# A graph and attention layer on one Trainium2 core: x's transposes in eight PSUM banks, edge slots in three pieces

## The chip, the core and the metric

The kernel runs on one core of one Trainium2 chip. The metric is the device time of one execution in microseconds (us). Three timed runs of the kernel before gave 1199.53, 1200.68 and 1201.06 us, median 1200.68.

## What is computed

`x` has 625 rows of 768 numbers. One layer is computed: a layer norm, a graph convolution over 20,625 edges, an attention of 12 heads with 266 random features, an output projection, and then a mixture of 16 experts in which each row uses one shared expert and up to three chosen ones. The change touches only the beginning. Cut to that, the reference is:

```python
xn = layernorm(x)
deg = segment_sum(ones, dst); norm = deg**-0.5[src] * deg**-0.5[dst]
gnn = segment_sum((xn @ gnn_W)[src] * norm, dst) + gnn_b
q, k, v = split(xn @ W_qkv)
q1, k1 = softmax_features(q), softmax_features(k)
mix = (q1 @ (k1.T @ v)) / (q1 @ sum(k1)) @ W_proj + b_proj
x = x + gnn + mix
x = x + experts(layernorm(x))
```

## The kernel before, in words

There is no scheduler: each engine (PE, ACT, DVE, POOL, SP) has its own list of instructions, written by hand, and the engines wait for each other on semaphores. Every product is made of three matmuls, (high, high), (high, low) and (low, high): ACT copies a matrix to a rounded high half and DVE subtracts that to get the low half (`split_high`, `split_low`, L499 to L508).

**Transposes of x.** After the norm, PE transposes xn into PSUM in eight groups: six groups "c" with the first four row tiles of one 128-column chunk, and two groups "l", ("l", 0) and ("l", 4), with the last row tile of four and of two chunks (`turn_tokens`, L462). ACT copies each group to `xhi` (L1380, L1383), then DVE subtracts it to `xlo` (`x_lower`, L973) and frees its bank. `groups` (L321) gives each key a bank in turn, out of the list it is handed; `fill` (L396) makes PE wait, before it writes a group into a bank, until the use before it has been freed. The x groups share banks 5, 6 and 7. Behind them PE transposes two small things, `lnrow` (group "lt", L1628) and `prow` (group "pt", L1634), and then starts the product h = xn @ gnn_W (`rows_times("h")`, L1659 to L1676), in two halves s of five row tiles. `rows_times("v")` follows in the same form, and then the columns of k (`columns_times`, L1678). The matmuls of the second half of v need `split_low(dve, "v", 1)`.

**Edge slots.** Each of 125 partitions holds 165 edges. DVE marks each edge's bucket of 25 (`ehot`), runs a scan over the marks (`erun`, L896), and sends totals to PE, which sums them (`bucket_ranks`, L1652, between the fourth and the fifth group of h). From PE's answer DVE makes each edge's slot in a table: `slots_of(a, b)` (L918) does so for columns a to b of the 165, with 25 instructions into `epos`, one reduction (L925), nine small instructions in a chain, each waiting for the one before (`link`), the last of which is the copy to `eslot` (L935) that raises `eslot_ok`. POOL then scatters the 165 columns into DRAM, one indirect DMA each (L731), and waits for `eslot_ok` before the first column of each piece. SP waits for it too, before it loads W_q. DVE's order in this stretch is:

```python
slots_of(*HALVES_OF_EDGES[0])
split_low(dve, "v", 0)
slots_of(*HALVES_OF_EDGES[1])
tile_regions()
split_biases()
split_low(dve, "v", 1)
```

The scattered table is loaded back (L640) long after, when PE projects the attention's output, and DVE makes one-hot matrices of it (L963) from which PE counts the adjacency matrix.

Of the kernel before, what the change touches and what calls it, by code (L numbers as in the profile page):

```python
# [31 lines left out]
ET = EDGES // TP  # L32
# [4 lines left out]
EDGE_RANGE = 32768.0  # L37
IN_FLIGHT = 8
WARM = 92
FIRST_EDGES = 28  # L40
HALVES_OF_EDGES = [(0, FIRST_EDGES), (FIRST_EDGES, ET)]
OFFSETS = 16
REGION = [512 * (r // 4) + TP * (r % 4) for r in range(BUCKETS)]
COUNT_BANKS = (BUCKETS + 3) // 4
# [65 lines left out]
def gps_kernel(nc, x, src, dst, gnn_w, gnn_b, w_qkv, w_proj, b_proj, proj_mat, gate_w, gate_b,  # L110
# [3 lines left out]
    with ctx:  # L114
# [206 lines left out]
        def groups(keys, banks):  # L321
            nonlocal turn
            for key in keys:
                b = banks[turn % len(banks)]
                turn += 1
                uses[b] += 1
                plan[key] = (b, uses[b])

        R3, R8 = [5, 6, 7], list(range(8))
        T8 = [("c", c) for c in range(C)] + [("l", 0), ("l", 4)]  # L330
        groups([("xt",) + k for k in T8], R3)
        groups([("lt", 0)], R3)
        groups([("pt", 0)], R3)
        groups([("h", i, s) for s in range(2) for i in range(NT)], R3)
# [80 lines left out]
        def sems(names):  # L415
            return [sem(n) for n in names.split()]
# [15 lines left out]
        iota_r_ok, epad_ok, etot_ok, eslot_ok, eoffs_ok, bias_ok, eye_ok, oh_ready, oh_free, counted, adj_ok, adjsum_ok = sems(  # L432
            "iota_r_ok epad_ok etot_ok eslot_ok eoffs_ok bias_ok eye_ok oh_ready oh_free counted adj_ok adjsum_ok")
# [18 lines left out]
        def done(eng, key):  # L452

            b, n = plan[key]
            eng.wait_ge(full[b], n)
# [48 lines left out]
        def split_low(dve, name, s):  # L504

            dve.wait_ge(half_hi, HALVES.index((name, s)) + 1)
            dve.tensor_tensor(wlow[name][:, :, 384 * s:384 * s + 384], wraw[name][:, :, 384 * s:384 * s + 384],
                              high_half(name, s)[:, :, :].bitcast(F32), ALU.subtract).then_inc(half_lo, 1)  # L508
# [67 lines left out]
        def _(sp):  # L576
# [6 lines left out]
            def load_qkv(name, a):  # L583
                sp.dma_start(wraw[name][:, :, :], w_qkv.rearrange("(c p) n -> p c n", c=C)[:, :, a:a + D]).then_inc(ld_w[name], 16)
# [14 lines left out]
            sp.dma_start(bias_f[:, F // 8:], fc2_b.rearrange("e (j c) -> (e j) c", j=8)).then_inc(ld_bf, 16)  # L599

            done(sp, ("xt", "l", 4))
            sp.wait_ge(eslot_ok, 2)
            load_qkv("q", 0)
            sp.wait_ge(eoffs_ok, 1)
            sp.dma_start(region_dram.rearrange("(p w) -> p w", p=128), eoffs[:, :]).then_inc(st_offs, 16)
# [85 lines left out]
        def _(pool):  # L691
# [31 lines left out]

            pool.wait_ge(st_epad, 16)
            for k in range(ET):
                for n, (a, b) in enumerate(HALVES_OF_EDGES):
                    if k == a:
                        pool.wait_ge(eslot_ok, n + 1)
                if k >= IN_FLIGHT:
                    pool.wait_ge(st_edges[k % IN_FLIGHT], 16 * (k // IN_FLIGHT))  # L730
                pool.indirect_dma_start(out=edge_dram, out_offset=bass.IndirectOffsetOnAxis(ap=eslot[:, k:k + 1], axis=0),  # L731
                                        in_=epair[:, k, :].bitcast(I32), in_offset=None).then_inc(st_edges[k % IN_FLIGHT], 16)
# [126 lines left out]
        def _(dve):  # L859
# [46 lines left out]
            def edge_slots():  # L906

                ps = read(dve, ("er", 0))
                link(dve.tensor_scalar(etiles[:, :], ps[:, 32:32 + BUCKETS], 1.0 / 128, 127.0 / 128 - 0.5 + 0.5 / 128, ALU.mult, ALU.add))
                link(dve.tensor_scalar(etiles[:, :], etiles[:, :], ROUND, ROUND, ALU.add, ALU.subtract))  # L910
                link(dve.tensor_tensor_scan(eend[:, :], ones[:, 0:BUCKETS], etiles[:, :], 0.0, ALU.mult, ALU.add))
                link(dve.tensor_tensor(efrom[:, :], eend[:, :], etiles[:, :], ALU.subtract))
                emptied(dve.scalar_tensor_tensor(out=efrom[0:TP, :], in0=efrom[0:TP, :], scalar=EDGE_RANGE, in1=ps[0:TP, 0:BUCKETS],
                                                 op0=ALU.mult, op1=ALU.add), ("er", 0))
                taken(dve, ("er", 0))
                link(dve.tensor_tensor(efrom[0:TP, 1:BUCKETS], efrom[0:TP, 1:BUCKETS], elast[:, 0:BUCKETS - 1], ALU.subtract))

            def slots_of(a, b):  # L918

                for n in range(BUCKETS):  # L920
                    last = dve.scalar_tensor_tensor(out=epos[:, n, a:b], in0=erun[:, n, a:b], scalar=efrom[0:TP, n:n + 1], in1=ehot[:, n, a:b],
                                                    op0=ALU.add, op1=ALU.mult)
                link(last)
                value, base_of, quo_of = evalue[:, a:b], ebase[:, a:b], equo[:, a:b]
                link(dve.tensor_reduce(value, epos[:, :, a:b].rearrange("p b k -> p k b"), AX.X, ALU.add))  # L925

                link(dve.tensor_scalar(base_of, value, 1.0 / EDGE_RANGE, -0.5 - 0.5 / EDGE_RANGE, ALU.mult, ALU.add))
                link(dve.tensor_scalar(base_of, base_of, ROUND, ROUND, ALU.add, ALU.subtract))
                link(dve.scalar_tensor_tensor(out=value, in0=base_of, scalar=-EDGE_RANGE, in1=value, op0=ALU.mult, op1=ALU.add))
                link(dve.tensor_scalar(quo_of, value, 1.0 / 128, -0.5 - 0.5 / 128, ALU.mult, ALU.add))  # L930
                link(dve.tensor_scalar(quo_of, quo_of, ROUND, ROUND, ALU.add, ALU.subtract))
                link(dve.scalar_tensor_tensor(out=base_of, in0=quo_of, scalar=1.0 - 128 * ET_TILES, in1=base_of, op0=ALU.mult, op1=ALU.add))
                link(dve.scalar_tensor_tensor(out=value, in0=value, scalar=float(ET_TILES), in1=base_of, op0=ALU.mult, op1=ALU.add))
                link(dve.tensor_scalar(value, value, -float(ET_TILES), None, ALU.add))
                dve.tensor_copy(eslot[:, a:b], value).then_inc(eslot_ok, 1)  # L935
# [68 lines left out]
            bucket_totals()  # L1004
            split_low(dve, "h", 1)
            edge_slots()
            slots_of(*HALVES_OF_EDGES[0])
            split_low(dve, "v", 0)
            slots_of(*HALVES_OF_EDGES[1])
            tile_regions()  # L1010
            split_biases()
            split_low(dve, "v", 1)
# [1025 lines left out]
```

## Time and profile before

| | |
|---|---|
| median of three runs | 1200.68 us |
| profiled execution, own time | 1206.77 us |
| its span | 1205.1 us |
| mean granted PE clock | 0.979 |
| PE busy | 1151.7 us (96%) |
| DVE busy | 761.0 us (63%) |
| ACT busy | 659.1 us (55%) |
| POOL busy | 490.4 us (41%) |

The profiled execution's own time is 1.67 us above its span and 6.09 us above the median of the timed runs. All the rows further down are of that execution. The first 30 us are the norm and x's transposes, 30 to 63 us the product h, 63 to 95 us v, 95 to 190 us k, q and their features, 190 to 316 us the attention, 316 to 385 us the output projection with the counting of the edges, and the experts fill the rest.

### The profile page before, as it was taken

The numbers are of one execution on the slowest core, as the hardware profiler recorded it, in microseconds if no ns is written. First come the engines' busy times: TensorE is split into PE (matmuls) and PEld (weight loads), VectorE is DVE, ScalarE is ACT, GpSimd is POOL, SyncE is SP. The second block draws the span as 40 slices with busy tenths as digits, with TensorE's granted clock in tenths as the row PEclk, the third lists the DMA queues.
The fourth block names the chain that finished last, engine by engine and source line by source line (L and its number), as shares of the span: only waits on it lengthen the run. The fifth ranks groups of instructions, "written<-read, shape, count | busy, mean of one in ns | idle before, by whom it ended". The sixth has DMA issues, their size and how long they took to land.

```text
span 1205.1 us, 20725 instructions
## 1 busy us (share of the span) xinstructions
PE 1151.7 (96%) x6465; PEld 1014.8 (84%) x6493; DVE 761.0 (63%) x1191; ACT 659.1 (55%) x1040; POOL 490.4 (41%) x340
## 2 busy tenths in 40 slices
PE   6999999999889999999999999999999999999985
PEld 5999898777666678888999988888889989998874
DVE  7862643256487656525866865747675896666973
ACT  3222673155500145336876684857776977486953
POOL 1188888788811000443632521312443642222511
PEclk8999999799999999999999999999999999999988
DMA  9030005140300330146596574565775959377933
GB/s 311 17 88 2 3 2 142 26 163 2 82 13 3 104 116 28 27 116 212 223 350 231 188 291 148 207 205 187 300 272 204 373 183 336 86 279 282 349 115 98
DMA packets 63089, 191.71 MB, mean 159 GB/s; under 512 B 14316, under 2 KB 15383, under 8 KB 63045
## 3 DMA queue, kind: packets, MB, share of 16 engines
q1 hardware_dynamic: 51316, 172.86, 39.3%
q0 software_dynamic: 11728, 18.27, 8.5%
q8 instruction: 27, 0.44, 0.2%
q14 instruction: 18, 0.14, 0.0%
HBM read 178.74 MB, written 15.09 MB: 161 GB/s over the span
## 4 chain that ended last, share of the span: by engine, by line
PE 81%; DVE 5%; ACT 4%; DMA 4%; issue 3%; POOL 1%; ACTq 0%; SPq 0%; DVEq 0%; another core or an unknown queue 0%; POOLq 0%
PE banks L1939 25%; PE banks L1923 23%; PE banks L1672 5%; PE banks L1689 4%; PE banks L1739 3%; PE banks L1837 3%; PE banks L1859 3%; PE banks L1704 3%; PE banks L1907 3%; PE banks L1761 2%; PE banks L1911 2%; DMA out<-ysb,sidx 2%; ACT kfeat L1432 2%; PE banks L1900 1%; PE banks L1750 1%
## 5 line engine op out<-in xcount | busy, mean ns | idle before, releaser
L731 POOL DMA_INDIRECT edge_dram<-epair,eslot x165 | 224.4, 1360 | 99.4 <-issue 99.4
L795 POOL DMA_INDIRECT out<-ysb,sidx x27 | 126.3, 4679 | 233.1 <-issue 198.6
L521 ACT ACTIVATE w2hi<-w2raw 128x1536 fp32r<-128x1536 f32 x96 | 139.1, 1483 | 90.2 <-DMA w2raw<-in_L_ffn_fc_w 80.0
L534 DVE TENSOR_TENSOR w2lo<-w2raw,w2hi 128x1536 fp32r<-128x1536 f32 x96 | 164.5, 1753 | 25.9 <-ACT w2hi L521 23.8
L1939 PE MATMUL banks<-w2hi,hthi 128*128 128x384 f32 x624 | 161.8, 340 | 0.1
L1939 PE MATMUL banks<-w2hi,htlo 128*128 128x384 f32 x624 | 159.2, 336 | 0.0
L1939 PE MATMUL banks<-w2lo,hthi 128*128 128x384 f32 x624 | 158.9, 335 | 0.0
L521 ACT ACTIVATE w1hi<-w1raw 128x1536 fp32r<-128x1536 f32 x96 | 137.6, 1495 | 29.2 <-DMA w1raw<-in_L_ffn_fc_w 25.7
L534 DVE TENSOR_TENSOR w1lo<-w1raw,w1hi 128x1536 fp32r<-128x1536 f32 x80 | 144.1, 1865 | 0.0
L1923 PE MATMUL banks<-w1hi,xthi 128*128 128x512 f32 x486 | 139.7, 396 | 2.6 <-POOL w1lo L534 2.6
L1923 PE MATMUL banks<-w1lo,xthi 128*128 128x512 f32 x486 | 136.9, 390 | 0.0
L1923 PE MATMUL banks<-w1hi,xtlo 128*128 128x512 f32 x486 | 136.6, 389 | 0.0
L1525 ACT ACTIVATE hid<-banks,lnwb 128x128 f32<-128x128 f32 x324 | 116.0, 488 | 32.2 <-PE banks L1907 31.1
L867 DVE BATCH_NORM_STATS2 st<-hid 128x6 f32<-128x512 f32 x81 | 50.7, 681 | 117.8 <-ACT hid L1536 117.8
L1939 PEld LDWEIGHTS banks<-w2lo,hthi 128*128 128x128 f32 x624 | 113.5, 189 | 0.0
L1939 PEld LDWEIGHTS banks<-w2hi,htlo 128*128 128x128 f32 x624 | 113.0, 188 | 0.0
L1939 PEld LDWEIGHTS banks<-w2hi,hthi 128*128 128x128 f32 x624 | 111.8, 189 | 0.6 <-issue 0.6
L1923 PEld LDWEIGHTS banks<-w1lo,xthi 128*128 128x128 f32 x486 | 91.3, 188 | 19.3
L1923 PEld LDWEIGHTS banks<-w1hi,xtlo 128*128 128x128 f32 x486 | 91.3, 188 | 19.2
L1923 PEld LDWEIGHTS banks<-w1hi,xthi 128*128 128x128 f32 x486 | 89.0, 188 | 19.8 <-POOL w1lo L534 2.2
L1211 DVE TENSOR_TENSOR htlo<-hid,hthi 128x1536 fp32r<-128x1536 f32 x26 | 45.7, 1756 | 85.4 <-ACT hthi L1531 85.4
L534 POOL TENSOR_TENSOR w1lo<-w1raw,w1hi 128x1536 fp32r<-128x1536 f32 x16 | 60.2, 3765 | 28.9 <-remote 17.2
(347 smaller groups left out, 1867.8 us busy)
## 6 DMA issues: line engine op xcount, KB each, us to landing
w1raw<-in_L_ffn_fc_w SPq DMA_DIRECT2D x96, 768.0 KB
w2raw<-in_L_ffn_fc_w SPq DMA_DIRECT2D x96, 768.0 KB, 6.6
xs<-in_x SPq DMA_DIRECT2D x10, 336.0 KB
edge_dram<-epair,eslot POOLq DMA_INDIRECT x165
wg<-in_L_gnn_W SPq DMA_DIRECT2D x1, 2304.0 KB, 12.6
wv<-in_L_mix_W_qkv SPq DMA_DIRECT2D x1, 2304.0 KB, 13.8
wk<-in_L_mix_W_qkv SPq DMA_DIRECT2D x1, 2304.0 KB, 17.7
wq<-in_L_mix_W_qkv SPq DMA_DIRECT2D x1, 2304.0 KB, 9.0
```

The costliest lines, as they stand in the source:

```text
L521: act.activation(unit(w2hi if second else w1hi, second, u), unit(w2raw if second else w1raw, second, u), ACT.Copy).then_inc(w2_hi if secon ...
L534: eng.tensor_tensor(unit(w2lo if second else w1lo, second, u), unit(w2raw if second else w1raw, second, u), unit(w2hi if second else w1hi, ...
L731: pool.indirect_dma_start(out=edge_dram, out_offset=bass.IndirectOffsetOnAxis(ap=eslot[:, k:k + 1], axis=0), in_=epair[:, k, :].bitcast(I3 ...
L795: pool.indirect_dma_start(out=out, out_offset=bass.IndirectOffsetOnAxis(ap=sidx[:, 0:1], axis=0), in_=ysb[:, :], in_offset=None, bounds_ch ...
L867: last = dve.bn_stats(st6[0:p, n, :], rows[:, n * step:(n + 1) * step])
L1211: dve.tensor_tensor(lo[:, :, :].rearrange("p c t -> p (c t)"), hid[:, :], hi[:, :, :].rearrange("p c t -> p (c t)").bitcast(F32), ALU.subt ...
L1525: last = act.activation(hid[:, 128 * c:128 * c + 128], tr_ps[c // 4][:, 128 * (c % 4):128 * (c % 4) + 128], ACT.Identity, scale=lnw[:, bas ...
L1672: last = pe.matmul(ps[0:TP, 0:384], a[:, c, t], w, start=c == 0 and k == 0, stop=c == C - 1 and k == 2)
L1689: last = pe.matmul(ps[:, 0:b - a + b % 2], w, xt_[:, c, a:b + b % 2], start=c == 0 and k == 0, stop=c == C - 1 and k == 2)
L1704: filled(pe.matmul(ps[0:TP, 0:M], of[r:r + HD, h // 2, TP * i:TP * i + TP], projt[r:r + HD, :], start=True, stop=True), (name, i, h))
L1923: last = pe.matmul(hid_ps[n][:, :], a[:, c, :], w[:, c, 512 * n:512 * n + 512], start=c == 0 and k == 0, stop=False)
L1939: last = pe.matmul(y_ps[s][:, 0:384], a[:, c, :], w[:, c, 384 * s:384 * s + 384], start=c == 0 and k == 0, stop=False)
```

## The change

The eight groups of x's transposes get banks 0 to 7, one each. The second piece of the edge slots, columns 28 to 165, is split in two, 28 to 96 and 96 to 165, one right behind the other; POOL waits at columns 0, 28 and 96, and SP's wait before the load of W_q is for the third piece. One line fewer stands at the top of the file, so the lines from 41 to 1006 have numbers lower by one.

```diff
-FIRST_EDGES = 28
-HALVES_OF_EDGES = [(0, FIRST_EDGES), (FIRST_EDGES, ET)]
+PARTS_OF_EDGES = [(0, 28), (28, 96), (96, ET)]
...
-        groups([("xt",) + k for k in T8], R3)
+        groups([("xt",) + k for k in T8], R8)
...
-            sp.wait_ge(eslot_ok, 2)
+            sp.wait_ge(eslot_ok, len(PARTS_OF_EDGES))
...
-                for n, (a, b) in enumerate(HALVES_OF_EDGES):
+                for n, (a, b) in enumerate(PARTS_OF_EDGES):
...
-            slots_of(*HALVES_OF_EDGES[0])
+            slots_of(*PARTS_OF_EDGES[0])
             split_low(dve, "v", 0)
-            slots_of(*HALVES_OF_EDGES[1])
+            slots_of(*PARTS_OF_EDGES[1])
+            slots_of(*PARTS_OF_EDGES[2])
             tile_regions()
             split_biases()
             split_low(dve, "v", 1)
```

Two places show it in the engines' lists. On PE, from the first transpose of the last group "c" on, with the semaphores that each instruction waits for (`free5` is raised when bank 5 is freed), before:

```order
L472 MATMUL banks<-ident,xn 128x125 [waits xn_ok,free7]
L472 MATMUL banks<-ident,xn 128x125 [waits xn_dve]
L472 MATMUL banks<-ident,xn 128x125 [waits xn_ok]
L472 MATMUL banks<-ident,xn 128x125 [waits xn_dve]
L472 MATMUL banks<-ident,xn 128x125 [waits xn_ok,free5]
L472 MATMUL banks<-ident,xn 128x125 [waits xn_ok] x3
L472 MATMUL banks<-ident,xn 128x125 [waits xn_ok,free6]
L472 MATMUL banks<-ident,xn 128x125 [waits xn_ok]
L1628 MATMUL banks<-ident,lnrow 128x96 [waits free7,ld_ln]
```

and now, from the same transpose on:

```order
L471 MATMUL banks<-ident,xn 128x125 [waits xn_ok]
L471 MATMUL banks<-ident,xn 128x125 [waits xn_dve]
L471 MATMUL banks<-ident,xn 128x125 [waits xn_ok] x6
L1628 MATMUL banks<-ident,lnrow 128x96 [waits free7,ld_ln]
L1628 MATMUL banks<-ident,lnrow 128x96 x3
L1634 MATMUL banks<-ident,prow 128x112 [waits free5,ld_proj]
```

No transpose of x waits for a bank any more; `lnrow` goes into bank 7 as before, whose last user was the sixth group and is now the eighth.

On DVE, from the low half of v's first half on (`wvlo<-wv,hi_v`), before:

```order
L507 TENSOR_TENSOR wvlo<-wv,hi_v 128x6x384
L921 SCALAR_TENSOR_TENSOR epos<-erun,efrom,ehot 125x137 x25
L925 TENSOR_REDUCE evalue<-epos 125x137
L927 TENSOR_SCALAR ebase<-evalue 125x137
L928 TENSOR_SCALAR ebase<-ebase 125x137
L929 SCALAR_TENSOR_TENSOR evalue<-ebase,evalue 125x137
L930 TENSOR_SCALAR equo<-evalue 125x137
L931 TENSOR_SCALAR equo<-equo 125x137
L932 SCALAR_TENSOR_TENSOR ebase<-equo,ebase 125x137
L933 SCALAR_TENSOR_TENSOR evalue<-evalue,ebase 125x137
L934 TENSOR_SCALAR evalue<-evalue 125x137
L935 CAST eslot<-evalue 125x137
```

and now, from the instruction behind that low half on:

```order
L920 SCALAR_TENSOR_TENSOR epos<-erun,efrom,ehot 125x68 x25
L924 TENSOR_REDUCE evalue<-epos 125x68
L926 TENSOR_SCALAR ebase<-evalue 125x68
L927 TENSOR_SCALAR ebase<-ebase 125x68
L928 SCALAR_TENSOR_TENSOR evalue<-ebase,evalue 125x68
L929 TENSOR_SCALAR equo<-evalue 125x68
L930 TENSOR_SCALAR equo<-equo 125x68
L931 SCALAR_TENSOR_TENSOR ebase<-equo,ebase 125x68
L932 SCALAR_TENSOR_TENSOR evalue<-evalue,ebase 125x68
L933 TENSOR_SCALAR evalue<-evalue 125x68
L934 CAST eslot<-evalue 125x68
L920 SCALAR_TENSOR_TENSOR epos<-erun,efrom,ehot 125x69 x25
```

The ten rows of the piece of 69 columns follow, and then the same rows as before: DVE has 35 instructions more, ahead of the low half of v's second half.

## Rows read from the trace of the kernel before

**Rows 1.** The page: busy time of each engine, and the chain that ended last.

```profile
PE 1151.7 (96%) x6465; PEld 1014.8 (84%) x6493; DVE 761.0 (63%) x1191; ACT 659.1 (55%) x1040; POOL 490.4 (41%) x340
...
PE 81%; DVE 5%; ACT 4%; DMA 4%; issue 3%; POOL 1%; ACTq 0%; SPq 0%; DVEq 0%; another core or an unknown queue 0%; POOLq 0%
```

**Rows 2.** The chain in order of time, 28 to 95 us: start, length, what.

```profile
28.54 0.87 PE banks L1628 x4
...
30.18 13.87 PE banks L1672 x72
...
44.08 50.65 PE banks L1672 x288
```

**Rows 3.** Timeline, PE and DVE at x's transposes: start, length, instruction, idle before.

```profile
18.66 1.29 PE L472 MATMUL banks<-ident,xn 125*128 125x125 f32 x10 [0.48 <-ACT xn L1371]
...
23.26 1.84 DVE L978 TENSOR_TENSOR xlo<-banks,xhi 128x500 fp32r<-128x500 f32 x3
23.98 4.56 PE L472 MATMUL banks<-ident,xn 125*128 125x125 f32 x18 [4.04 <-DVE xlo L978]
...
28.49 1.00 DVE L981 TENSOR_TENSOR xlo<-banks,xhi 128x500 fp32r<-128x500 f32 x2
```

**Rows 4.** Timeline, DVE, 44 to 79 us.

```profile
44.12 0.18 DVE L909 TENSOR_SCALAR etiles<-banks 128x25 f32<-128x25 f32 x1 [3.01 <-PE banks L1657]
...
45.47 4.06 DVE L921 SCALAR_TENSOR_TENSOR epos<-erun,efrom,ehot 125x28 f32<-125x28 bf16 x25
...
52.88 2.55 DVE L507 TENSOR_TENSOR wvlo<-wv,hi_v 128x2304 fp32r<-128x2304 f32 x1
55.35 6.88 DVE L921 SCALAR_TENSOR_TENSOR epos<-erun,efrom,ehot 125x137 f32<-125x137 bf16 x25
...
70.21 0.58 DVE L931 TENSOR_SCALAR equo<-equo 125x137 f32<-125x137 f32 x1
...
72.19 0.14 DVE L939 TENSOR_TENSOR etcmp<-eend,etile 128x50 f32<-128x50 f32 x1
...
76.09 2.55 DVE L507 TENSOR_TENSOR wvlo<-wv,hi_a 128x2304 fp32r<-128x2304 f32 x1
```

**Rows 5.** Timeline, PE, at the first matmul of v's second half.

```profile
78.54 0.34 PE L1672 MATMUL banks<-hi_v,xlo 128*125 128x384 f32 x1
78.72 0.42 PE L1672 MATMUL banks<-hi_a,xhi 128*125 128x384 f32 x1
```

**Rows 6.** PE by stretches: from:to, us, busy (instructions), granted clock, DMA share, GB/s.

```profile
22.00:23.00 1.00, 0.00 (x0) 0.64 0.99 381
32.00:33.00 1.00, 1.00 (x6) 0.74 0.05 18
223.50:244.00 20.50, 18.71 (x84) 0.50 0.30 90
```

**Rows 7.** The chain in order of time, 200 to 245 us.

```profile
200.88 4.61 PE banks L1739 x40
205.49 0.65 PE banks L1704 x4
...
223.45 3.34 PE banks L1739 x16
...
227.97 9.78 PE banks L1739 x40
```

**Rows 8.** The scatters as a group of the page; timeline, POOL and SP.

```profile
L731 POOL DMA_INDIRECT edge_dram<-epair,eslot x165 | 224.4, 1360 | 99.4 <-issue 99.4
...
57.00 6.30 POOL L731 DMA_INDIRECT edge_dram<-epair,eslot  x1 [0.31 <-issue]
...
326.57 1.83 POOL L731 DMA_INDIRECT edge_dram<-epair,eslot  x1 [0.30 <-issue]
...
330.01 0.34 SPq L640 DMA_DIRECT2D etab<-edge_dram  x1
```

**Rows 9.** Timeline, DVE's first use of that table.

```profile
336.90 0.34 DVE L1143 CAST ecode<-etab 128x370 f16<-128x370 f32 x1
```

## The prediction

> **What bounds the kernel now.** I read the page first: PE is busy 96% of the span and holds 81% of the chain that ended last [rows 1]. Whatever delays PE while it has no slack therefore moves the end. Next the chain in order of time, for the stretch that the change touches: from 30.18 us on it is matmuls alone, 72 and then 288 of h and v up to 94.73 us, 0.176 us each, with no idle time between them [rows 2]. Then the timelines of that stretch, and there the reader is to see two things. Before 30 us PE waits 4.04 us for DVE to free a bank [rows 3]; that is the wait which the new banks take away. And at 78.7 us PE comes to the second half of v with no gap, 0.18 us behind the matmul before it [rows 5], while DVE ends the low half that it needs at 76.09 + 2.55 = 78.64 us [rows 4]. The slack there is 0.08 us. DVE has no idle time between 44.12 us, when PE's answer on the edges arrives, and that moment [rows 4], so each microsecond that is added to DVE's list in between is a microsecond for which PE stands still.
>
> **Term 1, x's transposes: -0.3 us.** Today the 4th group waits for DVE to take the 1st. With a bank for each, PE makes groups 4 to 6 right behind the first three, some 1.4 us at the rate of the row at 18.66 us, and ACT copies them early [rows 3]. What is late next is DVE. It comes to the first group at 23.26 us and takes 0.61 us for each of six (three in 1.84) and 1.00 us for the last two: it ends at about 27.9 us, today at 29.5 us [rows 3]. PE gains less than these 1.5 us, since `lnrow`'s group now has to wait for the eighth group's bank, at 27.9 to 28.0 us. Today it starts at 28.54 us [rows 2], so h starts 0.5 us earlier. PE then runs at the half level of its clock, 1.2 GHz: the granted clock fell in the 23rd microsecond, after PE had stood still from 19.95 us, and rose to full in the 33rd [rows 6]. If the rise stays where it is, the time won is spent at half speed and is worth half: 0.3 us. Bounds: 0, and the 1.5 us that DVE gains, for a start at full clock. The earlier scan on DVE is worth nothing by itself: DVE waits 3.01 us for PE's answer all the same [rows 4], and that answer comes with h's fourth group, so 0.3 us earlier.
>
> **Term 2, the edge slots: +4.7 us.** A piece of 28 columns lasts from 45.47 to 52.88 us, 7.41 us; one of 137 columns from 55.35 to 72.19 us, 16.84 us [rows 4]. That is 0.0865 us a column and 4.99 us that a piece costs however small it is. Its 25 instructions into `epos` alone show it: 4.06 us for 28 columns, 6.88 us for 137, so 0.13 us of each do not depend on its width. Two pieces of 68 and 69 columns hold the same columns and pay the fixed part twice: 7.41 + 40 x 0.0865 = 10.87 and 7.41 + 41 x 0.0865 = 10.96, together 21.83 us against 16.84, +4.99 us. Bounds: among the nine small instructions of the 137 columns some lasted longer than their like, as the one at 70.21 us with 0.58 us [rows 4]; some 0.5 us of the piece may be such chance, and either goes or comes twice. That gives 4.5 to 5.7 us. DVE then ends the low half of v at 78.64 - 0.3 + 4.99 = 83.33 us, and PE goes on 0.08 us later, at 83.4 us, where today it does at 78.72: 4.7 us later, term 1 taken off already. PE arrives at 78.4 us, so it stands still for 5.0 us. Behind the wait on DVE is the low half of k, another 2.5 us, due only 16 us later. PE's list is in order, so all that follows moves with it; I find no wait further on that a PE later by 5 us would shorten, since what PE waits for hangs on PE's own results.
>
> **Term 3, the clock behind that stand: +1.9 us.** The trace of before has no stand of PE in dense matmuls of this length. The nearest is the one of 4.04 us at 19.95 us [rows 3]: the clock went to half during it [rows 6]. What it cost afterwards I take from the nearest dense work: from `lnrow` at 28.54 us [rows 2] to the rise at about 32.3 us PE worked 3.8 us at half clock, so it lost 1.9 us. Bounds: nothing, if the clock holds, and half of all that lay between PE's return at 23.98 us and the rise, 8.3 us, so 4.2 us.
>
> **Terms at nothing.** POOL gets piece 2 earlier, yet has no use for it: at 1.36 us or more for a scatter, and the second of them at 57 us, its first 28 columns reach past 92 us [rows 8], and piece 2 is there at 72 us already. The price of the scatters is that DVE's runs of `epos` hold them up: the second scatter took 6.30 us while such a run was on, until 1.1 us past its end at 62.2 us [rows 8, 4]. Two runs of 5.1 us instead of one of 6.9 add some 4 us to the 165 scatters. The Trainium skill ("SBUF — State Buffer", section "Who interferes with whom") infers that a vector instruction with two inputs does not stop descriptor generation; by that the scatters would not get longer at all, but the row of 6.30 us says otherwise, and I go by the row. The scatters now end at 328.4 us, the table's load is issued at 330.01 us [rows 8] and DVE reads it at 336.90 us [rows 9]. Later by 4 us, that load is issued at 334 us, against a DVE that comes 6.6 us later, at 343.5 us: 9.5 us for the load, today 6.9. SP's load of W_q is issued 5 us later, some 35 us before its first use. PE's order does not change.
>
> **The sum.** +4.7 + 1.9 = +6.6 us: for the profiled execution 1206.77 + 6.6 = 1213.4 us, and as that stands 6.09 us above the median of the timed runs, 1200.68 + 6.6 = **1207.3 us** for the median.
>
> **The rivals.**
>
> *A. The stand leaves the clock up.* For it: PE comes out of 50 us of dense matmuls [rows 2], not out of transposes. Against it: the row at 22 us [rows 6]. Then the sum is 4.7 us: 1205.4 us.
>
> *B. The slow stretch further on goes away (not slower).* From 223.5 to 244 us PE works at half clock, at 0.91 of its time busy [rows 6], in the sums over keys and values. There 16 + 4 + 40 matmuls and the 4 behind them take 14.3 us, from 223.45 to 237.75, where at full clock they would take 1.84 + 0.65 + 4.61 + 0.65 = 7.75 us [rows 7]; with the transposes and projections up to 244 us it is 8.4 us. If this work, 6.6 us later, keeps its clock, the change returns 8.4 us: 1198.9 us, and 1197.0 together with A. It decides where the clock holds for at least 16 of the 20 us. The Trainium skill ("TensorE: Matmul & The Clock Gate", "Part 1: The HAM clock gate") says that the moments at which the clock changes follow a beat of its own and not the kernel's start, so that the cost varies by run; by that rule the runs of before should lie apart by up to 8.4 us. Three of them lie within 1.53 us, which is why I give this little.
>
> *C. It falls one group of heads earlier there.* Two heads more at half clock add 4.6 + 0.65, 5.3 us: 1212.6 us.
>
> *D. The change does not reach PE.* Then DVE would have to make up 5 us before 78.6 us, or PE to have something else to do. The rows give 0.08 us of slack; only a start of DVE's part that is earlier by 5 us could hide it, and it hangs on PE's fourth group. 1200.4 us.
>
> *E. The edge path becomes the bound.* The load takes at most the 6.9 us that it has today; PE's delay adds 6.6 us. So the scatters would have to get at least 6.6 us longer, where I count 4. At each microsecond above that, 1 us: 1209.3 us for 2 more.
>
> **How the numbers follow.** Forecast 0.62, A 0.16, B 0.10 (0.06 by itself, 0.04 with A), C 0.05, D 0.05, E 0.02. A measurement of this kernel tells about 0.2% from no change, 2.4 us. Slower by more: the forecast, A, C and E, 0.85. Within it: D and B by itself, 0.11. Faster: B with A, 0.04. The range takes the bounds of the terms together: at the low end 4.5 - 1.5 + 0 = +3.0, 1203.7 us; at the high end 5.7 - 0 + 4.2 = +9.9, 1210.6 us. It holds the forecast, A and E, 0.80.
>
> **What would show each step.** Term 1: PE's wait of 4 us inside the transposes is gone, the 8th `xlo` ends near 28 us and h starts near 29.7 us. Term 2: the two pieces last 10.9 us each, the low half of v ends at about 83.3 us, and the list of PE's waits has a new first entry, DVE `wvlo`, of 5 us; the chain runs through DVE's `epos` there. Term 3: a granted clock of 0.5 for some 4 us behind 83 us. The sum is wrong if PE's wait for `wvlo` is under 4 us, or if the share of half clock between 200 and 250 us is another than now. I am wrong altogether if v's second half starts before 80 us.

## The result, and the profile after

The changed kernel takes 1194.8 us (median of five runs, 1193.33 to 1196.4), the kernel before beside it 1201.06 us (five runs, 1199.53 to 1203.41). The ratio is 0.994, 95% interval 0.9924 to 0.9955. The change made the kernel faster by 6 us where 6.6 us of loss were forecast. The profiled execution took 1196.4 us by itself, 1.6 us above its median.

Nearly every local step of the forecast is in the trace of the changed kernel all the same. First the timeline of PE at x's transposes, and of DVE beside it (columns: start, length, instruction, idle time before and what ended it):

```profile
18.32 2.57 PE L471 MATMUL banks<-ident,xn 125*128 125x125 f32 x22 [0.49 <-ACT xn L1371]
23.25 0.86 PE L471 MATMUL banks<-ident,xn 125*128 125x125 f32 x6 [2.36 <-ACT xn L1371]
27.61 0.87 PE L1628 MATMUL banks<-ident,lnrow 96*128 96x96 f32 x4 [3.51 <-DVE xlo L980]
```
```profile
26.47 1.00 DVE L980 TENSOR_TENSOR xlo<-banks,xhi 128x500 fp32r<-128x500 f32 x2
```

The 4.04 us for a bank [rows 3] are gone, the last `xlo` ends at 27.5 us, PE now waits 3.51 us for it ahead of `lnrow`, and h starts at 29.05 us (29.7 forecast). Next DVE's slots: what was one piece of 137 columns [rows 4] is now two.

```profile
54.81 5.12 DVE L920 SCALAR_TENSOR_TENSOR epos<-erun,efrom,ehot 125x68 f32<-125x68 bf16 x25
...
65.79 5.13 DVE L920 SCALAR_TENSOR_TENSOR epos<-erun,efrom,ehot 125x69 f32<-125x69 bf16 x25
...
80.80 2.55 DVE L506 TENSOR_TENSOR wvlo<-wv,hi_a 128x2304 fp32r<-128x2304 f32 x1
```

They last 10.98 and some 10.8 us. PE pays for it where [rows 5] had no gap, and works at half clock behind the stand (the second fence is PE by stretches: from:to, us, busy, granted clock, DMA share, GB/s):

```profile
83.41 0.68 PE L1672 MATMUL banks<-hi_a,xhi 128*125 128x384 f32 x1 [5.07 <-DVE wvlo L506]
```
```profile
80.50:87.00 6.50, 3.59 (x11) 0.50 0.84 279
223.50:244.00 20.50, 18.78 (x144) 0.92 0.50 164
237.50:240.80 3.30, 3.30 (x18) 0.50 1.01 389
```

k's first matmul comes at 100.97 us, before at 94.57: 6.4 us later, where 6.6 us were forecast. Then the loss vanishes. The stretch that had a granted clock of 0.50 over 20.5 us before [rows 6] now has 0.92. The first start of each stage on PE, in us, tells where the time comes back:

| stage of PE | before | after | difference |
|---|---|---|---|
| v, second half | 78.72 | 83.41 | +4.7 |
| k | 94.57 | 100.97 | +6.4 |
| key features | 131.28 | 137.69 | +6.4 |
| q | 151.35 | 155.27 | +3.9 |
| sums over keys and values | 195.55 | 199.45 | +3.9 |
| attention | 239.67 | 236.05 | -3.6 |
| projection | 316.80 | 307.88 | -8.9 |
| first count matmul | 338.89 | 330.05 | -8.8 |
| end of the span | 1205.1 | 1194.7 | -10.4 |

The last row is larger than the 6.3 us between the medians, since the profiled execution of before was 6.09 us above its own median. One thing in the trace went against a step of the forecast. GpSimd's second scatter took 6.30 us before [rows 8] and was to be joined by more such losses; now it is short. GpSimd's timeline, and the group on the page (busy, mean ns):

```profile
56.46 1.19 POOL L730 DMA_INDIRECT edge_dram<-epair,eslot  x1 [0.31 <-issue]
...
321.28 1.77 POOL L730 DMA_INDIRECT edge_dram<-epair,eslot  x1 [0.30 <-issue]
```
```profile
L730 POOL DMA_INDIRECT edge_dram<-epair,eslot x165 | 219.6, 1331 | 98.9 <-issue 98.9
```

165 scatters cost 4.8 us less than before, not 4 us more. At this point three theories stood, by the names that they have in the expectations: "clock", the later start shortens PE's own stages further on (rival B and more of its kind); "pieces", the finer pieces change GpSimd's scatters and free what waits for them (the path of rival E, but with another sign); and "banks".

### The profile page after: what moved, and what is told of

The parts are those of the page before. It is cut to its first block, busy times and chain, and to the rows that moved or that the text cites. A ratio compares the mean times of both kernels' runs of the same rounds, so it can differ in the third digit from the quotient of the medians.

```text
span 1194.7 us, 20786 instructions
## 1 busy us (share of the span) xinstructions
PE 1142.5 (96%) x6492; PEld 1008.1 (84%) x6493; DVE 762.3 (64%) x1226; ACT 657.6 (55%) x1040; POOL 450.2 (38%) x340
## 4 chain that ended last, share of the span: by engine, by line
PE 78%; DVE 9%; issue 4%; ACT 4%; DMA 3%; POOL 1%; ACTq 0%; SPq 0%; DVEq 0%; POOLq 0%
PE banks L1939 25%; PE banks L1923 24%; PE banks L1689 3%; PE banks L1704 3%; PE banks L1837 3%; PE banks L1859 3%; PE banks L1672 3%; PE banks L1907 2%; PE banks L1761 2%; PE banks L1739 2%; PE banks L1911 2%; ACT kfeat L1432 2%; DMA out<-ysb,sidx 2%; PE banks L1900 1%; DVE oh L962 1%
## 5 line engine op out<-in xcount | busy, mean ns | idle before, releaser
L730 POOL DMA_INDIRECT edge_dram<-epair,eslot x165 | 219.6, 1331 | 98.9 <-issue 98.9
L794 POOL DMA_INDIRECT out<-ysb,sidx x27 | 84.9, 3143 | 264.8 <-issue 231.0
L533 DVE TENSOR_TENSOR w1lo<-w1raw,w1hi 128x1536 fp32r<-128x1536 f32 x80 | 141.6, 1834 | 0.1
```

Source lines behind the costliest of these rows:

```text
L533: eng.tensor_tensor(unit(w2lo if second else w1lo, second, u), unit(w2raw if second else w1raw, second, u), unit(w2hi if second else w1hi, ...
L794: pool.indirect_dma_start(out=out, out_offset=bass.IndirectOffsetOnAxis(ap=sidx[:, 0:1], axis=0), in_=ysb[:, :], in_offset=None, bounds_ch ...
```

## The experiments

Each series ran on one chip, with the kernel before timed beside it; the ratios are to that kernel in that series.

### First series: undo each part, and delay alone

before_again is the kernel before. banks_only has the eight banks alone:

```diff
-        groups([("xt",) + k for k in T8], R3)
+        groups([("xt",) + k for k in T8], R8)
```

pieces_only has the three pieces alone (all lines of the diff but that one). delay5 keeps two pieces and gives DVE one idle reduction behind the second, whose result nobody reads (meant to take 4.9 us; the traces show 4.70 to 4.71 us):

```diff
             slots_of(*HALVES_OF_EDGES[1])
+            link(dve.tensor_reduce(equo[:, 0:101], epos[:, :, 0:101].rearrange("p b k -> p k b"), AX.X, ALU.add))
             tile_regions()
```

> The kernel before, unchanged, for a second profile of it and the granted clock of each timed run. Theory 'clock': the place of the half-clock stretch in the sums over keys (223.5 to 244 us in the first profile) follows the schedule and is there again in most runs, with about 20 us at clock 0.5; median 1201 us. Theory 'scatter between runs': the stretch was an accident of one profiled execution (its own time, 1206.77 us, was above all five timed runs); the new profile lacks it or has it elsewhere, and then it can't be what the change gained in the medians.

> The eight banks alone, the edge slots in two pieces as before. PE starts h about 1 us earlier at half clock, and comes to v's second half 0.55 us earlier. DVE's low half is ready 0.55 us earlier too, so PE does not wait there. Theory 'clock' (the gain comes from where later work falls against changes of the clock, so it takes a shift of several us): 1200.1 to 1201.2 us, ratio 0.999 to 1.000, half-clock stretch still there. Theory 'banks' (the gain is in the banks): 1195 us, ratio 0.995.

> Three pieces alone, x's transposes in three banks as before. Theory 'clock' and theory 'pieces' alike: PE stands still for 5.0 us at v's second half, k starts 7 us later than before, and the time is nevertheless 1195 us, ratio 0.995. Theory 'banks': +6.9 us, 1208 us, ratio 1.006.

> The kernel before with one more DVE instruction behind the second piece of the slots, a reduction of some 4.9 us over what is in epos, whose result nothing uses. Slots, scatters and banks are as before; PE stands still for 4.9 us at v's second half. Theory 'clock' (it is only the shift that counts): as pieces_only, 1195 us, ratio 0.995. Theory 'pieces' (finer pieces change POOL's scatters, and that frees the later stages): no gain, 1200.7 + 4.9 + 1.9 = 1207.5 us, ratio 1.005.

| kernel | median us | ratio | 95% interval |
|---|---|---|---|
| before_again | 1205.11 | 0.9994 | 0.9963 to 1.0026 |
| banks_only | 1204.08 | 1.0007 | 0.9975 to 1.0040 |
| pieces_only | 1215.55 | 1.0076 | 1.0047 to 1.0105 |
| delay5 | 1217.61 | 1.0108 | 1.0065 to 1.0151 |

The banks are worth nothing. But the pieces, the part that ought to carry the gain, lost 0.8%, where both "clock" and "pieces" had 0.995, and the pure delay 1.1%: in this series my forecast looked right. The stretch at half clock is there in all four traces, for 17.1 us in before_again and banks_only and for 20.5 us in pieces_only and delay5, where PE comes 6 to 7 us later. So a later start doesn't remove it, against the theory "clock". The kernel before itself lay between 1198.26 and 1213.69 us here, against 1199.53 to 1203.41 in the comparison. So the change itself had to be run again, and beside a delay.

### Second and third series: the change again, and delay alone again

after_again and after_b are the changed kernel, before_b, banks_b and delay5_b those of the first series; banks_delay5 has the eight banks and the reduction.

> The changed kernel once more, beside the kernel before, with a second profile. Each half of the change alone gave no gain (1.0007 and 1.0076), so either the two together do what neither does, or the gain is not the change's. Theory 'together': as measured first, ratio 0.994, no half-clock stretch of 17 to 20 us in the sums over keys, and 17.6 us from the first key feature matmul to q, where all others show 20.1 to 20.9. Theory 'adds up' (the shares add, +0.0007 and +0.0076): ratio 1.005 to 1.010, with the long half-clock stretch and 20 to 21 us there, and the first comparison was not a fair one.

> Eight banks and, in place of the finer pieces, the one added DVE reduction of 4.9 us. Theory 'together' by the shift alone: as the changed kernel, ratio 0.994. Theory 'adds up': 1.0007 x 1.0108, ratio 1.008 to 1.012.

> The kernel before, a third profile, in one series with the three below. So far the stages with many small matmuls were long (20.1 to 20.9 us from the first key feature matmul to q, 43.3 to 45.2 us of sums over keys) in every kernel without both parts of the change, and short (17.6 and 36.6 us) in both kernels with eight banks and a shift of 5 us; but all but one of the long ones were measured in one series on one chip, and both short ones in others. Theory 'chip': the stages' length goes with the chip, so all four of this series agree on it. Theory 'kernel': this one is long (20 and 43 us) on any chip.

> Eight banks alone. Theory 'kernel': long stages, ratio 0.999 to 1.001. Theory 'chip': as the others of the series.

> The 4.9 us reduction on DVE alone, three banks. Theory 'kernel' with both parts needed: long stages, ratio 1.008 to 1.012 as in its first series. Theory 'shift' (the shift of 5 us by itself shortens the stages wherever they can be short): short stages, 17.6 and 36.6 us, ratio 1.000. Theory 'chip': as the others of the series.

> The changed kernel, third profile. Theory 'kernel': short stages (17.6 and 36.6 us), ratio 0.994 to 0.997 on any chip. Theory 'chip': as the others of the series; if long here, ratio near 1.008.

| kernel | median us | ratio | 95% interval |
|---|---|---|---|
| after_again | 1195.45 | 0.9959 | 0.9944 to 0.9975 |
| banks_delay5 | 1200.22 | 1.0001 | 0.9986 to 1.0016 |
| before_b | 1200.21 | 1.0000 | 0.9985 to 1.0014 |
| banks_b | 1199.95 | 0.9993 | 0.9980 to 1.0005 |
| delay5_b | 1199.83 | 0.9999 | 0.9988 to 1.0010 |
| after_b | 1193.79 | 0.9946 | 0.9926 to 0.9966 |

Here the added reduction, which makes the low half of v 5.1 us late, is free, and the change gains. (For banks_delay5 neither of the expected ratios came, not 0.994 and not 1.008 to 1.012.) The four traces of the third series are so alike that the reason can be read off. First starts on PE:

| stage of PE | before_b | banks_b | delay5_b | after_b |
|---|---|---|---|---|
| k | 92.76 | 93.74 | 100.51 | 100.29 |
| key features | 129.47 | 130.45 | 137.22 | 137.01 |
| sums over keys and values | 191.25 | 192.22 | 198.99 | 198.79 |
| projection | 299.70 | 300.70 | 307.40 | 307.21 |
| first count matmul | 333.81 | 334.80 | 335.53 | 329.38 |
| end of the span | 1196.8 | 1197.7 | 1198.1 | 1191.6 |

From k to the projection nothing moves: delay5_b is 7.7 us behind before_b all the way. At the first count matmul 6.0 of these are gone; the 1.7 us that stay are those by which its table comes later (its load is issued at 330.13 us, in before_b at 328.42 us). The first count matmul is where PE waits for the edges. banks_b is 1.0 us behind before_b in every row, the last ones too. Its h starts 0.2 us earlier, but its clock is still at half then (granted 0.50 from 27.0 to 31.3 us, in before_b 1.00), so PE's answer on the edges comes 0.8 us later and both chains with it. PE's timelines at the first count matmul, of before_b, delay5_b and after_b in turn:

```profile
320.45 1.51 PE L1837 MATMUL banks<-wp,aot 128*125 128x384 f32 x4
333.81 2.27 PE L1821 MATMUL banks<-oh 128*125 128x125 bf16 x16 [11.86 <-DVE oh L963]
```
```profile
328.15 1.50 PE L1838 MATMUL banks<-wp,aot 128*125 128x384 f32 x4
335.53 2.31 PE L1822 MATMUL banks<-oh 128*125 128x125 bf16 x16 [5.87 <-DVE oh L963]
```
```profile
327.96 1.50 PE L1837 MATMUL banks<-wp,aot 128*125 128x384 f32 x4
329.38 2.21 PE L1821 MATMUL banks<-oh 128*125 128x125 bf16 x16
```

before_b has 11.86 us of slack on PE: whatever makes PE alone later up to here is paid out of it. After the delay 5.87 us of it are left, and in after_b nothing. Follow it back in before_b. DVE waits for the load of the table, SP issued that load behind the last scatter, and the chain of waits (start, length, what) runs from DVE's first slots through GpSimd to the end. DVE, SP, chain:

```profile
330.82 1.62 DVE L1143 CAST ecode<-etab 128x370 f16<-128x370 f32 x1 [10.95 <-DMA etab<-edge_dram]
```
```profile
328.42 0.34 SPq L640 DMA_DIRECT2D etab<-edge_dram  x1
```
```profile
47.75 1.47 DVE evalue L925
...
52.20 2.68 POOL edge_dram L731
...
55.19 6.30 POOL edge_dram L731
```

In after_b the same places read (DVE, SP, then GpSimd's second scatter):

```profile
327.31 0.69 DVE L1143 CAST ecode<-etab 128x370 f16<-128x370 f32 x1
```
```profile
323.98 0.34 SPq L639 DMA_DIRECT2D etab<-edge_dram  x1
```
```profile
56.05 1.20 POOL L730 DMA_INDIRECT edge_dram<-epair,eslot  x1 [0.31 <-issue]
```

The load is issued 4.44 us earlier than in before_b, the count matmul comes 4.43 us earlier, and the span is 5.2 us shorter. Against delay5_b, which has the same stand on PE, it is 6.15 us for the load and 6.15 us for the matmul. That the numbers agree so well is in part chance, for in after_b the table is not what PE waits for any more. The chain of after_b, in order of time, comes through PE's projection and DVE's last addition to `xs`:

```profile
307.21 19.60 PE banks L1837 x60
326.81 0.02 issue
326.84 0.56 DVE xs L1136
327.39 0.62 DVE ecode L1143
```

The load lands 2.4 us after its issue, at some 326.4 us, and DVE comes to it 0.9 us later, straight from that addition. So PE's own path is the bound again, with 0.9 us between the two chains, and it sets the size of the gain: 11.86 us of slack less the 7.5 us by which PE now comes later leave some 4.4 us. The shorter edge chain is what lets PE use them. Of the 6.15 us for the load, 5.1 us are the second scatter: 6.30 us against 1.20. In all eight traces with the piece of 137 columns (before, before_again, banks_only, delay5, banks_delay5, before_b, banks_b, delay5_b) the longest scatter lasts 6.30 to 6.31 us; in all twelve with 68 and 69 columns it lasts 3.34 to 3.57 us. From the first scatter's start to the last one's it is 269.6 to 274.0 us in the eight, and 263.8 to 267.8 us in the ten of the twelve that have no other delay put in.

### Fourth and fifth series: each chain by itself

The reading was to be tried by four kernels. pieces_b is pieces_only once more. edges_late is the changed kernel with GpSimd held ahead of its second scatter, so that the edge chain loses what it won:

```diff
                     if k == a:
                         pool.wait_ge(eslot_ok, n + 1)
+                if k == 1:
+                    done(pool, ("h", NT - 1, 1))
```

v_early takes PE's stand away and leaves the scatters:

```diff
             slots_of(*PARTS_OF_EDGES[1])
+            split_low(dve, "v", 1)
             slots_of(*PARTS_OF_EDGES[2])
             tile_regions()
             split_biases()
-            split_low(dve, "v", 1)
```

edges_early is v_early with the head of the edge chain earlier too:

```diff
-            rows_times("h", {3: bucket_ranks})
+            rows_times("h", {2: bucket_ranks})
```

> The kernel before with the edge slots in three pieces of 28, 68 and 69 columns, x's transposes still in three banks. Theory 1 (the bound is the edge chain: GpSimd's 165 scatters, the load of the edge table, the one-hots; TensorE waits for it at its first count matmul): the second scatter takes 1.2 us and not 6.3, the last ends near 322 us and not near 327, and the first count matmul comes near 329.5 us where the kernel before in the last series had it at 333.8. TensorE's stand of 5 us ahead of v's second half is there all the same. Time 5 us under the kernel before, ratio near 0.995, as with both parts; the eight banks are worth nothing. Theory 2 (the gain needs the later start and the eight banks together, through the fill of TensorE's queue in the stages of the key features and of the sums over keys and values): no gain, ratio 1.000 to 1.008. If a stretch of 17 us or more at half the clock shows in the sums over keys and values, as in the first series, TensorE comes to its counts later than the table does and the run tells nothing of the edge chain.

> The changed kernel, with GpSimd held ahead of its second scatter until the last group of h's second half is in its bank (near 62.2 us; the scatter started at 56.05 us before). Nothing else moves, and TensorE waits for nothing new ahead of the counts. Theory 1 (edge chain): every scatter behind it comes 6.1 us later, the last ends near 328.5 us, the table is there near 332.5 us, the first count matmul comes near 335.5 us in place of 329.4, TensorE stands idle ahead of it for about 6 us, and the time is 5 to 6 us over the changed kernel: ratio to the kernel before near 1.000, no gain left. Theory 2 (TensorE's own stages carry the gain): the first count matmul stays within 2 us of 329.4 us, ratio near 0.995.

> The changed kernel with VectorE's split of v's second half between the second and the third piece of slots rather than behind the third, the tile regions and the biases. TensorE's stand of 5.1 us at 77.8 to 83.0 us and the half clock behind it go: k starts near 93.4 us in place of 100.3, and the projection near 300.3 us in place of 307.2. Theory 1 (edge chain): the first count matmul moves only until the table holds it, from 329.4 to about 328.2 us, TensorE stands idle ahead of it for some 5 us, and the time is 0.5 to 1.5 us under the changed kernel, ratio to the kernel before 0.994 to 0.995. Theory 2 (TensorE's time is what counts, as my prediction had it): the time is 6.9 us under the changed kernel, ratio near 0.989.

> As v_early, and TensorE makes the two matmuls that rank the buckets behind the third group of h's first half rather than the fourth, so that VectorE, which stood idle for 4.0 us until them, starts the slots some 3.1 us earlier, and GpSimd its scatters too. Theory 1 (edge chain, now shortened at its head, with TensorE's own path 7 us shorter): the last scatter ends near 319.3 us, the table is there near 323.3 us, the first count matmul comes near 325 us, and the time is 4 to 5 us under the changed kernel, ratio to the kernel before near 0.991: faster than both. Theory 2 (TensorE's time is what counts): the same as v_early, within 0.5 us. In both a slow stretch in the sums over keys and values may come back with TensorE's earlier start, which would take TensorE's 7 us away again.

> The changed kernel once more. The series so far are of two kinds. In the one (the first comparison, after_again, before_b to after_b) the kernel before keeps within 1195.5 and 1204.3 us and its stages between v and the projection last what they last in after_b: there the edge chain decides and the change is worth 0.5%. In the other (before_again to delay5, pieces_b to edges_early) the kernel before spreads from 1198 to 1215 us, TensorE needs 10 to 16 us more between the sums over keys and values and the projection, comes to its counts later than the edge table, and every us ahead of v's second half counts. In a series of the first kind I expect a ratio of 0.995 for this kernel; in one of the second 1.005 to 1.009, by pieces_b: there my prediction of a loss holds.

> The kernel v_early once more. In a series of the first kind, theory 1 (the edge chain is the bound): the projection starts near 300.3 us, the first count matmul only near 328.2 us, ratio to the kernel before 0.994 to 0.995, at most 1.5 us under the changed kernel. Theory 2 (TensorE's time counts everywhere): ratio near 0.989. In a series of the second kind: again near 1.000.

> The kernel edges_early once more. In a series of the first kind, theory 1: the first count matmul near 325 to 326 us, 3 us ahead of v_early's, ratio to the kernel before near 0.992, the fastest of the four. Theory 2: the same as v_early_b. In a series of the second kind: again near 1.000.

> The kernel edges_late once more. In a series of the first kind, theory 1: first count matmul near 335.5 us with some 6 us of idle time ahead of it, ratio to the kernel before near 1.000, the gain of the change gone by the edge chain alone. Theory 2: ratio near 0.995 as with the change. In a series of the second kind the count matmuls come later than the table and the ratio is that of after_c.

| kernel | fourth series: median, ratio | fifth series: median, ratio |
|---|---|---|
| changed kernel (after_c) | not run | 1216.97, 1.0110 (1.0092 to 1.0128) |
| pieces_b | 1214.96, 1.0089 (1.0054 to 1.0123) | not run |
| edges_late, edges_late_b | 1214.2, 1.0062 (1.0032 to 1.0093) | 1214.81, 1.0079 (1.0044 to 1.0115) |
| v_early, v_early_b | 1205.96, 1.0000 (0.9964 to 1.0036) | 1207.43, 1.0044 (1.0029 to 1.0059) |
| edges_early, edges_early_b | 1206.97, 1.0007 (0.9976 to 1.0038) | 1206.65, 1.0022 (1.0003 to 1.0041) |

Both series fell on one chip, and it is of the kind of the first series. The changed kernel itself is 1.1% slower there, by 13 us (a ratio of 1.005 to 1.009 was expected). So the sign of the change depends on the execution one looks at. What sets the kinds apart is the length of three stages of PE; I call the two the short and the long form (us, from the first starts):

| trace | key features | sums over keys and values | attention |
|---|---|---|---|
| before_b | 17.6 | 36.6 | 67.1 |
| after, after_again, after_b | 17.6 | 36.6 | 67.1 |
| before | 20.1 | 44.1 | 71.8 |
| before_again | 20.9 | 43.3 | 70.2 |
| v_early_b | 20.9 | 44.3 | 71.6 |
| after_c | 20.8 | 41.3 | 77.7 |

In the short form these stages agree within 0.1 us over the seven traces that have it (after, after_again, banks_delay5 and the four of the third series). In the long form PE needs 9 to 21 us more for the three together and arrives at the counts when the table is already there. In before_again, which has the kernel before in the long form, PE doesn't stand still ahead of its first count matmul at 334.94 us, and the span of 1197.4 us is within 0.6 us of before_b's: the longer stages have used up the slack. In after_c SP issued the load of the table at 322.32 us:

```profile
322.32 0.34 SPq L639 DMA_DIRECT2D etab<-edge_dram  x1
```

and the first count matmul came at 352.24 us. The edge chain has some 20 us of slack then, and PE's own path is the bound, as I had read it. The numbers fit: v_early_b is 9.5 us under after_c (1207.43 against 1216.97), where k starts 7.5 us earlier (93.37 against 100.91) and the three stages take 3.0 us less, and to hold the edge chain back costs nothing (edges_late_b 1.0079 against 1.0110, intervals that overlap). One number is left open: v_early_b has neither the stand nor a late table and is still 0.4% slower than the kernel before.

And **the profiled execution of before was of the long form**. ScalarE's sixty copies of the key features show it best; PE makes two matmuls for each. Of before, after_c, before_b and after, in turn:

```profile
132.09 19.89 ACT L1427 ACTIVATE kfeat<-banks 125x266 f32<-125x266 f32 x60 [0.28 <-PE banks L1704]
```
```profile
138.43 20.62 ACT L1427 ACTIVATE kfeat<-banks 125x266 f32<-125x266 f32 x60 [0.28 <-PE banks L1704]
```
```profile
130.28 17.21 ACT L1427 ACTIVATE kfeat<-banks 125x266 f32<-125x266 f32 x60 [0.28 <-PE banks L1704]
```
```profile
138.49 17.21 ACT L1427 ACTIVATE kfeat<-banks 125x266 f32<-125x266 f32 x60 [0.28 <-PE banks L1704]
```

The instructions of this stage and their order are the same in all four. Even in that execution the edge chain was near. The entry of the table's load among the DMA issues of before (size, us from issue to landing) is

```profile
etab<-edge_dram SPq DMA_DIRECT2D x1, 185.0 KB, 2.4
```

so the table was there at 332.4 us, 4.5 us before DVE read it [rows 9].

None of the ratios below 1 that were expected in the fourth series came. What these two series did not test: the edge chain as the bound under v_early, edges_early and edges_late. In none of their eight traces did PE stand still ahead of its first count matmul. edges_early_b's profiled execution came nearest to it (sums 38.5 us, attention 71.2 us, end of the span 1196.4 us), with the table's load issued at 321.48 us and the first count matmul at 332.51 us; the median of its runs is 1206.65 us. Whether v_early or edges_early beats the changed kernel where the middle is short was not tried. No kernel here was shown to be faster than the kernel before in both kinds.

## Why the prediction was wrong, point by point

- **Term 1, x's transposes (-0.3 us): the mechanism right, worth nothing.** The bank wait went and `xlo` ended early. banks_b measured 0.9993 (0.9980 to 1.0005); in its trace h starts 0.2 us earlier than in before_b and v's second half 0.95 us later, since the clock rose later.
- **Term 2, the edge slots (+4.7 us at v): right.** PE came back at 83.41 us (83.4 forecast) after 5.07 us (5.0).
- **Term 3, the clock (+1.9 us): right.** v's second half lasts 17.56 us to k, before 15.85: 1.7 us. Rival A fell.
- **The scatters get some 4 us longer: wrong, in the sign.** The step was to scale one long scatter with the number of runs of `epos`. They got 4.8 us shorter: a run of 137 columns holds a scatter for 6.30 us, one of 68 or 69 holds none for that long. The inference of the Trainium skill ("SBUF — State Buffer", "Who interferes with whom"), that an instruction with two inputs on VectorE does not stop descriptor generation, would have given the new runs right and the old one wrong. Neither it nor the row alone gave both.
- **"I find no wait further on that a PE later by 5 us would shorten": the step that failed.** There is one, at L1821, of 11.86 us in before_b; 7.5 us of it took up PE's delay, and the shorter edge chain let PE use the rest. It isn't in the trace of before, because that execution came to it 5 us late (338.89 us against 333.81). The text had signs of it. The load of the table was read as lasting up to the 6.9 us at which DVE used it, and it landed after 2.4 us; so the edge chain had only 4.5 us to spare there. And the profiled execution lay 6.09 us above the median. I carried that as a constant offset onto the sum. It was another form of the middle with another bound.
- **Rival B (the slow stretch goes, 0.10): what I saw, and not the cause.** The stretch of 20.5 us at half clock is gone in after, but it is absent in before_b too (3.4 us near 230), whose sums over keys and values start 4.3 us earlier than in before, not later. The half clock there lasts 3.4 us in all seven short traces and 3.4 to 20.5 us in the thirteen long ones, so it goes with the long form; the change didn't remove it. after_c keeps 10.2 us of half clock between 240 and 251 us in spite of the shift.
- **Rival E (the edge path becomes the bound, 0.02): the right place, read from the wrong execution.** In before_b the edge path was the bound already, by 11.86 us of PE's time. The change shortened it and made PE later, until PE was the bound again by 0.9 us.
- **Range and sign.** 1203.7 to 1210.6 us held the loss of 3.0 to 9.9 us. On the chip of the long form the change loses 13 us, more than the upper end; in the three series where the trace of the changed kernel is short it gains 4.8 to 6.5 us. That both signs occur was no case of mine.

The account of the gain is shown for its place (elsewhere ahead of the counts the traces of the third series differ by PE's stand, the clock behind it and up to 1.2 us in h) and for the part of the delay (0.9999). The nearest to a kernel that undoes the finer pieces alone is banks_delay5 beside after_again, on one chip: the same banks, a stand of PE at the same place (k at 100.93 and 100.34 us), and 4.8 us between their medians (1200.22 against 1195.45). PE waits for the table in the one (the row) and not in the other:

```profile
334.49 2.27 PE L1822 MATMUL banks<-oh 128*125 128x125 bf16 x16 [4.38 <-DVE oh L963]
```

A kernel that lengthens the second scatter and leaves all else was only timed where the edge chain has slack (edges_late). Nor was the kernel with the pieces alone timed in a series of the short form; that the banks add nothing there rests on banks_b.

## What to carry to other kernels

Hold the profiled execution's own time against the median of the timed runs before anything is read from its chain: where they differ by more than the effect at issue, the chain may be that of another bound, and a second profile costs less than a wrong sum. That they agree proves little: before_again took 1199.09 us in the long form, and its chain doesn't wait for the table either. So compare the same stage in several traces, and read for each side chain how long its result lies ready before it is used. A long chain on a side engine (here 165 scatters from 52 to 327 us) can bound a kernel whose main engine is busy 96% of the time; look at where the two meet, and for how long the main one waits there. And a change that helps one chain and hurts the other, as this one does, has the sign of whichever is late: it should be judged on more than one chip.

## What the runs showed of the hardware beyond that

- The long form. ScalarE's copies of 125x266 start every 0.27 us in the short form, all sixty of them. In the long form the first 14 to 26 do too; from then on the steps between starts are mostly by turns 0.29 us and, in the mean of a trace, 0.45 to 0.48 us, with no other work of ScalarE between them. So the long form begins within this stage. In after_c the granted clock over these copies is 1.00. In the sums over keys and values a group of 40 matmuls lasts 4.58 to 4.68 us in after_b throughout; in after_c the first four do too, and then a gap appears for which the profile names nothing but "issue", and behind it slower groups and, from 240 us on, the half clock. PE's timeline of after_c:

```profile
223.31 4.58 PE L1739 MATMUL banks<-vext,kfeat 125*128 125x65 f32 x40
228.47 4.69 PE L1739 MATMUL banks<-vext,kfeat 125*128 125x65 f32 x39
233.44 0.22 PE L1739 MATMUL banks<-vext,kfeat 125*128 125x65 f32 x1 [0.29 <-issue]
234.24 4.89 PE L1739 MATMUL banks<-vext,kfeat 125*128 125x65 f32 x40
```

 The gap comes first and the clock falls behind it; and the copies of the key features are slow at full clock already, some 90 us earlier. So the clock is not where the long form begins. Its cause stays open. It goes with the chip or the moment and not with the kernel: all traces of the first, fourth and fifth series have the slow copies, none of the second and third has, and the first comparison has one of each (before long, after short).
- A scatter that starts beside the wide run of two-input instructions on VectorE (25 of 125x137 in 6.88 us) ends only 1.07 us after the run is over: 6.30 us, eight times out of eight. Beside runs of 125x68 (25 in 5.12 us) scatters last 1.19 to 1.31 us. Between 69 and 137 columns nothing was measured, and what decides isn't settled. It isn't the run of `epos` alone: the subtractions of low halves (two inputs of 128x2304, 2.55 us) hold scatters too. In all twenty traces the first scatter ends 1.26 us behind the end of such a subtraction, and every other one of the first sixty that lasts over 2.1 us beside one ends 1.05 to 1.06 us behind it. GpSimd and DVE of after_b:

```profile
80.66 3.35 POOL L730 DMA_INDIRECT edge_dram<-epair,eslot  x1 [0.30 <-issue]
84.31 2.16 POOL L730 DMA_INDIRECT edge_dram<-epair,eslot  x1 [0.31 <-issue]
```
```profile
80.39 2.55 DVE L506 TENSOR_TENSOR wvlo<-wv,hi_a 128x2304 fp32r<-128x2304 f32 x1
82.86 2.55 DVE L506 TENSOR_TENSOR wklo<-wk,hi_b 128x2304 fp32r<-128x2304 f32 x1
```
